# The second score products one row block later in the second feed-forward layer

## The reference

```
h = layernorm(x);  q = h,  k = v = ctx
i_pre, f_pre = 15 * tanh((concat(q, k, v) @ ifgate_w.T + ifgate_b) / 15)
log_d = cumsum(log_sigmoid(f)) differences + i_pre, causal mask
d = exp(log_d - rowmax);  s = (q @ k.T) / sqrt(32) * d
h = (s @ v) / (max(|sum(s)|, exp(-rowmax)) + 5e-5)
x1 = x + h * rsqrt(mean(h * h) + 1e-6) * (1 + outnorm_w)     # per head
z = layernorm(x1)
a = silu(z @ w1.T * w1_s) * (z @ w2.T * w2_s)                # 256 -> 1024
a = gelu(a @ h1.T * h1_s)                                    # 1024 -> 1024
a = gelu(a @ h2.T * h2_s)                                    # 1024 -> 1024
out = x1 + a @ w3.T * w3_s                                   # 1024 -> 256
```

## Time and profile before

| | |
|---|---|
| median of 3 runs | 768.38 us (767.89 to 768.53) |
| span of the profiled execution | 765.7 us, 15199 instructions |
| median less span | 2.7 us |
| TensorE busy | 756.8 us, 99% |
| VectorE busy | 543.2 us, 71% |
| ScalarE busy | 383.9 us, 50% |
| granted TensorE clock | 1.00 over the span |

### The profile page before, as it was taken

How to read it: one execution, slowest core, us unless ns; L and a number is a source line. 1 busy time by engine, 2 the same in 40 slices (tenths; PEclk the granted TensorE clock), 3 DMA queues, 4 the chain that set the end, 5 groups by cost and what they waited for, 6 DMA issues and landing times.

```text
span 765.7 us, 15199 instructions
## 1 busy us (share of the span) xinstructions
PE 756.8 (99%) x6296; PEld 628.7 (82%) x6296; DVE 543.2 (71%) x1295; ACT 383.9 (50%) x577; POOL 53.6 (7%) x67
## 2 busy tenths in 40 slices
PE   8999999999999999999999999999999999999998
PEld 4778888888897888878888888888889788888887
DVE  6878686586956968578675877658695684965554
ACT  3666455473355634556454554636435562435332
POOL 3400020000100020000200002000020000000000
PEclk9999999999999999999999999999999999999999
DMA  9392112200022010310005001230102100540540
GB/s 336 96 421 104 37 50 99 95 30 30 29 112 83 29 31 28 143 52 29 30 29 193 0 30 37 85 128 20 40 29 111 55 1 3 170 161 8 176 147 29
DMA packets 14616, 63.45 MB, mean 83 GB/s; under 512 B 2016, under 2 KB 2896, under 8 KB 11728
## 3 DMA queue, kind: packets, MB, share of 16 engines
q1 hardware_dynamic: 12960, 50.12, 18.7%
q0 software_dynamic: 1296, 11.53, 3.9%
q10 hardware_dynamic: 288, 0.79, 0.3%
HBM read 53.94 MB, written 8.50 MB: 82 GB/s over the span
## 4 chain that ended last, share of the span: by engine, by line
PE 80%; DVE 12%; ACT 1%; issue 1%; DVEq 0%; ACTq 0%
PE ps_f L1598 24%; PE ps_f L1599 24%; DVE decay L984 8%; PE ps_f L1564 8%; PE ps_f L1565 7%; PE ps_f L1638 4%; PE ps_f L1639 4%; PE ps_a L1504 2%; DVE decay L1000 2%; PE ps_a L1487 2%; PE ps_a L1339 1%; PE ps_a L1537 1%; DVE work L1158 1%; PE ps_a L1460 1%; PE ps_a L1453 1%
## 5 line engine op out<-in xcount | busy, mean ns | idle before, releaser
L1598 PE MATMUL ps_f<-h_hi,wgt 128*128 128x512 f32 x1024 | 401.7, 392 | 0.0
L1599 PE MATMUL ps_f<-h_lo,wgt 128*128 128x512 f32 x1024 | 398.9, 390 | 0.0
L1598 PEld LDWEIGHTS ps_f<-h_hi,wgt 128*128 128x128 f32 x1024 | 192.2, 188 | 41.7 <-issue 0.5
L1599 PEld LDWEIGHTS ps_f<-h_lo,wgt 128*128 128x128 f32 x1024 | 192.3, 188 | 38.8
L751 ACT ACTIVATE work<-ps_f,scl 128x512 f32<-128x512 f32 x128 | 87.5, 684 | 161.6 <-PE ps_f L1599 160.7
L1167 DVE TENSOR_TENSOR h_lo<-work,h_hi 128x512 fp32r<-128x512 f32 x128 | 86.4, 689 | 98.4 <-ACT h_hi L756 97.3
L1564 PE MATMUL ps_f<-h_hi,wgt 128*128 128x512 f32 x252 | 99.9, 396 | 0.2 <-DVE work L1158 0.2
L1565 PE MATMUL ps_f<-h_lo,wgt 128*128 128x512 f32 x252 | 98.8, 392 | 0.0
L738 ACT ACTIVATE work<-ps_f,scl 128x512 f32<-128x512 f32 x64 | 44.1, 689 | 97.4 <-PE ps_f L1565 96.5
L756 ACT ACTIVATE h_hi<-work 128x512 fp32r<-128x512 f32 x128 | 81.0, 632 | 4.1
L1158 DVE SCALAR_TENSOR_TENSOR work<-ps_f,scl,work 128x512 f32<-128x512 f32 x64 | 48.0, 750 | 46.3 <-ACT work L738 46.3
(11 more groups left out here) (214 smaller groups left out, 684.0 us busy)
## 6 DMA issues: line engine op xcount, KB each, us to landing
decay<-m_rows SPq DMA_DIRECT2D x14, 1024.0 KB, 6.6
decay<-w_cols SPq DMA_DIRECT2D x22, 512.0 KB, 4.2
wgt<-w_cols POOLq DMA_DIRECT2D x5, 1024.0 KB, 12.0
v_aug<-ctx_tok SPq DMA_DIRECT2D x8, 528.0 KB, 3.8
wgt<-w_cols POOLq DMA_DIRECT2D x2, 2048.0 KB, 13.6
x_kept<-xs SPq DMA_DIRECT2D x8, 512.0 KB, 2.6
xs<-x SPq DMA_DIRECT2D x7, 512.0 KB, 3.7
ctxT<-ctx_t SPq DMA_DIRECT2D x7, 512.0 KB, 3.3
```

What stands on the lines that cost most here:

```text
L1598: pe.matmul(ps_f[:, bank], w, moving(h_hi[layer][:, k], as_is), start=(k == 0), stop=False)
L1599: last = pe.matmul(ps_f[:, bank], w, moving(h_lo[layer][:, k], as_is), start=False, stop=(k == KH - 1))
```

## The change

TensorE issues the score products of the second sequence (b = 1) behind block 4 of the layer and not behind block 3. VectorE weighs them behind `lo` 2 and not behind `lo` 1.

```
@@ VectorE, batch @@
                 for m in range(KH):
                     lo(i, 0, m)
-                    if a_stage and m == 1:
+                    if a_stage and m == 2:
                         weigh_scores(j, 1)
@@ TensorE, batch @@
                 def after_2(m):
-                    if a_stage and m == 3:
+                    if a_stage and m == 4:
                         scores(j, 1)
```

## The result

The changed kernel takes 774.99 us (median of 5 runs, 774.64 to 775.61) against 768.09 us before (5 runs, 767.89 to 768.53): ratio 1.0091, 95% interval 1.0079 to 1.0103. It is 6.9 us slower; 5.2 us were forecast. The time lies in the range given, but above the forecast's own upper bound, 774.3. The profiled execution has a span of 773.0 us against 765.7, 7.3 us more. Its total is 774.99, so 2.0 us lie around the span, not the 2.7 that the prediction took.

What follows compares the result with a forecast made beforehand. TensorE's nearly packed list was taken as the bound. Per batch, 0.91 us added less 0.17 removed, taken as 0.75, times 7 gave +5.2 us: 768.4 to 773.6 us, range 772.4 to 775.6.

Steps and rivals of the forecast that it cites:

- own upper bound, 774.3: Top of the likeliest case's range from 773.2 us: block 4 stalls on gelu 0, state read in time; 82 in 100.
- the 2.7 that the prediction took: Time around the profiled span, 2.7 us, added to the forecast span of 770.9 to give 773.6 us.
- The bound: TensorE's list is nearly packed, busy 756.8 of 765.7 us; time gained or lost inside a batch moves the end equally.
- Removed, 0.17 us: Score products behind block 3 no longer wait for VectorE's first weighing: 0.17 us less per batch.
- Added, 0.91 us: Block 4 waits for ScalarE's gelu 0: 0.81 us late, release of 0.05 included, plus 0.10 restart, per batch.
- rival C: Block 4's weight load runs during the wait for gelu 0, so 7 x 0.65 us, 772.9 us; 4 in 100.
- The state, margin 0.25: VectorE's `take_state` shifts by 2.0 us but still ends in time for TensorE's `read_state`, margin 0.25 us.
- Rival B: VectorE's state comes late, a second TensorE wait ahead of `read_state` in batches 0 to 5: +1.8, 775.4 us; 8 in 100.
- Rival E: TensorE's granted clock falls from 2.4 to 1.2 GHz through the stalls: 26 us more, 800 us; 2 in 100.
- Rival D: Not slower: block 4 not held, or its loss given back at a hidden wait; -1.2 us, 767.2 us; 4 in 100.
- The sum: Loss of 0.91 less 0.17 per batch, taken as 0.75 us, in batches 0 to 6: +5.2 us.
- the weighing ends later: VectorE's second weighing was forecast to start at 264.3 us in batch 2, not at 261.73.

Runs made afterwards that it cites:

- tanh, new order: The changed kernel with tanh in place of gelu in the second FFN layer alone: 768.82 us, ratio 1.0008 against the kernel before.
- TensorE's half alone: The kernel before with only the score products moved behind block 4, VectorE still weighing them behind `lo` 1: 777.35 us, ratio 1.0127.

## Why the prediction was right, and where its size was off

*The bound.* TensorE's list is packed, and what it loses moves the end. Right: nowhere were the 0.74 us per batch given back.

*Removed, 0.17 us.* Right: all starts of L1487 at issue time, and 0.19 us less per batch where nothing else was changed in effect (tanh, new order).

*Added, 0.91 us.* Right in each part: release 0.05, lateness 0.81 (1.04 less 0.23), restart 0.12 for 0.10 (0.35 us to the second product, not 0.33). With the table load away it vanishes. The weight load ran after the wait (PEld idle 1.08 us up to 262.65), so rival C falls for this wait. That was the rule on reordering in the Trainium skill, page "TensorE: Matmul & The Clock Gate", section "Architectural detail: the array is 16× 32×32, not 1× 128×128"; these seven waits show no load pulled ahead.

*The state, margin 0.25.* Right: 0.26. Rival B's mechanism exists, as TensorE's half alone shows, but not in this kernel.

*The clock.* The granted clock stayed at 1.00 through all of it, the 2.4 GHz level. Rival E falls. Rival D falls with the seven waits.

*The sum.* 7 x 0.75 = 5.2 us was what the stalls cost. The term that was missing is a gap of 1.4 us at the many short products of batch 0, 1.7 us by the batch's length. The prediction counted what TensorE waits for by semaphore alone; "queued behind the waiting product is all of TensorE's list" was said, but not asked was whether that list arrives in time. It had worked out that the weighing ends later, by the right amount, and looked only at who reads its result.

*The range.* That 774.99 lies in it is luck in part. The forecast's own range, 773.2 to 774.3, does not reach it; the range went up to 775.6 for rival B, which did not happen, and the gap came in its place. Nor does that own range follow from the bounds given, which make 772.9 to 774.2. The 2.7 us around the span were 2.0: the span of the kernel before belongs to an execution of about 767.7 us. That moves the level, not the difference of 5.2.

*A sentence that was wrong.* "The transfers: none is issued in this part on SyncE's or GpSimd's list, and what waits for TensorE later moves with it." SyncE's load of the next ctxT waits on `s_qk`, which the moved score products raise, so it is released in this part, and it moved by far more than 0.75 us. In the 16 us from 76 us on (slices of 0.4 us) it runs in the slices from 82.8 us in the changed kernel:

```profile
GB/s 0 0 0 0 0 0 0 0 0 0 0 0 0 0 0 0 0 123 256 399 358 174 0 0 0 41 0 0 0 0 0 0 0 0 0 41 0 0 0 0
```

and from 78.0 us in the kernel before:

```profile
GB/s 0 0 0 0 0 102 215 410 410 174 0 0 0 0 0 0 0 41 0 0 0 0 0 0 0 0 0 41 0 0 0 0 0 0 0 0 0 0 0 0
```

Holding it back changed nothing (775.14), so no cost of the slip is shown; but a queue released by a moved step belongs in the list of what moves.

## What to carry to other kernels

A short wait ahead of a filler can be cheaper than the wait which the filler covers: before moving work out of a gap, look up when the next instruction behind it could start without it. Here the gap behind block 3 was 0.76 us until the end of gelu 0, and the filler of 1.1 us fitted it. When a wait of 0.17 us is to go, shorten what is waited for (two small instructions of VectorE moved behind it gave the whole of it) and leave the order alone. And where a long run of short products follows a semaphore wait, a later release can cost time although nobody is seen waiting for that semaphore: look at the packets of the instruction queue beside the run.

## What was not expected of the hardware

- TensorE can stand still 0.3 to 2.2 us inside a run of short products (about 9.7 ns from one to the next, 1.24 us for 128) with no semaphore in it. The point was the same 109th product in seven kernels, and went elsewhere when the list was shifted. It went on 2.3 to 2.9 us after a 16 KB packet of the instruction queue had started. Its places lie multiples of 256 instructions apart. In nine of eleven kernels the packet of batch 0 started 1.2 to 1.7 us after the semaphore wait ahead of the run could end; what delayed it in the two others, and in batch 1 of two kernels, stays open.
- A 128x128 float32 product on the identity is two products and two weight loads in the trace: 40 more of them are 80 rows and took 8.6 us, 0.2 us each.
